# A memset of its own between one box gather and the next on GpSimd

## The chip, the cores and the metric

The kernel runs on one core of a Trainium2 chip. The metric is device time in microseconds (us) of one execution. The engines are named as the profile names them: PE is TensorE's matmuls and PEld its weight loads, DVE is VectorE, ACT is ScalarE, POOL is GpSimd, SP is SyncE, which only issues transfers.

## The reference

Four convolution layers run one after the other on an image batch x of shape (4, 48, 256, 256). Each layer gets the normalised output of the one before and adds its input again. Cut to what matters here:

```python
# layer 0: 1x1 conv, 3x3 depthwise conv, product of q and k in the 8x8 Fourier domain, norm, 1x1 conv
# layer 1: 1x1 conv, mask in the 8x8 Fourier domain, 3x3 depthwise conv, gelu gate, 1x1 conv
# layer 2 (boxes):
integ = jnp.cumsum(jnp.cumsum(x, axis=-1), axis=-2)          # integral image
off_w, off_h, scale = ...                                    # from two small conv branches
A  = _grid_sample_border_bilinear(integ, off_tl)             # four corners of a box per pixel,
Bt = _grid_sample_border_bilinear(integ, off_tr)             # each a blend of 4 neighbours
Ct = _grid_sample_border_bilinear(integ, off_bl)
D  = _grid_sample_border_bilinear(integ, off_br)
return (A + D - Bt - Ct) / area
# layer 3: 1x1 conv, 3x3 depthwise conv, gelu gate, 1x1 conv, mask in the 8x8 Fourier domain
```

The corners of layer 2's boxes depend on the data, so their values are fetched from a table in device memory by index.

## The kernel before, in words

The 4 images are handled one at a time and an image is cut into 32 strips of 8 rows. For each image the program runs layer 0, layer 1, the integral image (written to memory as a table) and the front of layer 2, which computes for every pixel the table indices, the 16 blend weights and the reciprocal of the area and spills them to memory. Tiles of these stages have names that begin with `a_`, `b_`, `i_` and `c_`. Layer 3, with names `d_`, runs for all 4 images at the end.

The rest of layer 2, the box part (names `e_`, class `Boxes`), has no stage of its own. It is woven into other stages: the boxes of image 0 into layers 0 and 1 of image 1, those of image 1 into image 2's, those of image 2 into image 3's, and those of image 3 into layer 3 of images 0 to 2. Layer 0 and layer 1 of image 0, and layer 3 of image 3, have no boxes in them.

The box part works in units of 512 pixels, 128 units for an image, 64 in each layer 0 or layer 1 and 128 in the three box-carrying images of layer 3. For one unit:

- GpSimd issues 16 indirect DMAs (`gather` at L1674, `gather_unit` at L1689), each with one index per partition, into one of `nb` buffers `got`. `nb` is 2 in layers 0 and 1 and 4 in layer 3. GpSimd may start a unit when VectorE has finished the unit `nb` before it (semaphore `used`).
- VectorE waits for the 16 gathers (semaphore `gathered`), multiplies by the weights (L1727, twice), adds halves (L1733 twice, L1739, L1741, the last frees the buffer) and multiplies by the reciprocal area (L1744). These instructions stand at fixed places in VectorE's program between those of the host layer.
- TensorE transposes the result (L1769), VectorE adds the residual and takes statistics (L1782, L1784), SyncE stores it.

Every engine runs its own program in order. The engines meet only at semaphores and at the barrier between blocks (one block for each layer of each image). GpSimd has little else to do: some clears at a block's start (L875, L878), loads for the integral image (L1211) and the spills (L1417 to L1424). SyncE issues all other transfers; all transfers of the core, GpSimd's too, use the same 16 DMA engines. `ALU` rows in the listings below are register arithmetic.

Of the kernel before, what the change touches and what calls it, by code (L numbers as in the profile page):

```python
# [29 lines left out]
WIDE = 66  # L30
NPROD = 94
CREDIT = 8


def stack_planes():
# [104 lines left out]
def allocators(nc, ctx, tag):  # L140

    def sb(name, shape, dt=F32):
        return ctx.enter_context(nc.sbuf_tensor(f"{tag}_{name}", shape, dt))

    def pb(name, shape=(128, 512)):
        return ctx.enter_context(nc.psum_tensor(f"{tag}_{name}", list(shape), F32))
    return sb, pb


def semaphores(env, tag, names):  # L150


    keys = [("all" if n == "turn" else tag, n) for n in names]
    for k in keys:
        if k not in env.sems:
            env.sems[k] = env.ctx.enter_context(env.nc.semaphore("_".join(k)))
    return [env.sems[k] for k in keys]


def planes(t, b, c0, cn, row, rows, col=0, cols=WP):  # L160

    return t[ds(b, 1), c0:c0 + cn, ds(row, rows), col:col + cols].rearrange("a c y x -> (a c) y x")
# [108 lines left out]
def credit(eng, *sems, n=1):  # L271

    for s in sems:
        eng.sem_inc(s, n * CREDIT)

# [34 lines left out]
def first_stats(env, src, stats):  # L310
# [3 lines left out]
    with ExitStack() as ctx:  # L314
# [4 lines left out]
        with nc.Block() as block:  # L319
            @block.sync  # L320
            def _(sp):
                with sp.Fori(0, S // 2) as u:
                    for k in range(2):

                        sp.wait_ge(used, u * 2 + k + CREDIT - 1)
                        sp.dma_start(x[k][:], planes(src, 0, 0, CP, (u * 2 + k) * SROWS + 1, SROWS)).then_inc(loaded[k], 16)
# [13 lines left out]
def layer0(env, src, dst, p, b, boxes=None, stats=None):  # L340
# [6 lines left out]
    with ExitStack() as ctx:  # L347
# [37 lines left out]
        if stats is not None:  # L385
# [5 lines left out]
            loads_before = [U, U] + [0] * (B - 3)  # L391
        n_first = b * (4 * S) + CREDIT

        def pipeline(eng, begin, step):

            n0 = b * (4 * S) + CREDIT
            begin(n0)
# [16 lines left out]
        with nc.Block() as block:  # L416
            @block.sync
            def _(sp):
# [16 lines left out]
                def strip(u, k, load, more):  # L435
                    s = u * 2 + k
                    if more and stats is not None:
                        for i, t in enumerate(others):
                            sp.wait_ge(others_used, CREDIT + S + s * (B - 1) + i + 1)
                            sp.sem_inc(turn, 1)  # L440
                            sp.dma_start(t[:], planes(src, i + 1, 0, CP, (s + 1) * SROWS + 1, SROWS)).then_inc(others_loaded[i], 16)
                    if load:

                        sp.wait_ge(qk_ready, 2 * ((b * S + s + 1) * NQ + CREDIT))
                        sp.sem_inc(turn, 1)
# [882 lines left out]
class Spill:  # L1328


    def __init__(self, env):
        self.idx = env.nc.dram_tensor("spill_idx", [env.B, env.S, 128, NT * 4], I32, kind="Internal").ap()
        self.wt = env.nc.dram_tensor("spill_wt", [env.B, env.S, 128, NT * 16], F32, kind="Internal").ap()
        self.rec = env.nc.dram_tensor("spill_rec", [env.B, env.S, 128, NT * C], F32, kind="Internal").ap()
# [249 lines left out]
class Boxes:  # L1584
# [8 lines left out]
    def __init__(self, env, ctx, src, dst, table, spill, b, nb, ni):  # L1593
        self.env, self.src, self.dst, self.spill, self.b, self.nb, self.ni = env, src, dst, spill, b, nb, ni
        self.flat = table.rearrange("x y c -> (x y c)").rearrange("(n o) -> n o", o=1)
        sb, _ = allocators(env.nc, ctx, f"e{b}")
        self.got = [sb(f"got{i}", [128, 4, 4 * REC]) for i in range(nb)]
        self.idx = [sb(f"idx{i}", [128, self.HT * 4], I32) for i in range(ni)]
        self.wt = [sb(f"wt{i}", [128, self.HT * 16]) for i in range(2)]
        self.rec = [sb(f"rec{i}", [128, self.HT, C]) for i in range(2)]  # L1600
        self.out = [sb(f"out{i}", [CP, self.HROWS, WP]) for i in range(2)]
        self.box = sb("box", [128, 4, C])
        self.val = [sb(f"val{i}", [128, 4, WIDE]) for i in range(2)]
        (self.halved, self.used, self.v_ready, self.y_ready, self.res_ready, self.stats_done, self.turn_sem, self.cleared,
         aux0, aux1, x0, x1, s0, s1) = semaphores(env, "e", [
             "halved", "used", "v_ready", "y_ready", "res_ready", "stats_done", "turn", "cleared",
             "aux_loaded0", "aux_loaded1", "x_loaded0", "x_loaded1", "stored0", "stored1"])
        self.aux_loaded, self.x_loaded, self.stored = [aux0, aux1], [x0, x1], [s0, s1]
        self.idx_loaded = semaphores(env, "e", [f"idx_loaded{i}" for i in range(ni)])
        sems = semaphores(env, "e", [f"gathered{i}" for i in range(2 * nb)])  # L1610
        self.gathered = [sems[2 * i:2 * i + 2] for i in range(nb)]
        self.n0 = b * (4 * env.S) + CREDIT

        self.filled = [b * (2 * env.S) if i < 2 else 0 for i in range(nb)]
        self.listed = [b * env.S if i < 2 else 0 for i in range(ni)]
# [40 lines left out]
    def stores_done(self, sp, e):  # L1656
        for i in range(2):
            sp.wait_ge(self.stored[i], (self.b * self.env.S + e + 1) * 16)

    def gather(self, pool, lo, hi):  # L1660

        per = self.ni // 2
        with pool.Fori(lo // per, hi // per) as v:
            for slot in range(self.ni):
                pool.wait_ge(self.idx_loaded[slot], (self.listed[slot] + v + 1) * 16)
                for j in range(2):
                    q = (2 * slot + j) % self.nb

                    pool.wait_ge(self.used, self.n0 + v * (2 * self.ni) + (2 * slot + j) - self.nb + 1)
                    pool.sem_inc(self.turn_sem, 1)  # L1670
                    for t in range(4):
                        for c in range(4):
                            at = (j * 4 + t) * 4 + c
                            pool.indirect_dma_start(out=self.got[q][:, t, c * REC:(c + 1) * REC], out_offset=None, in_=self.flat,  # L1674
                                                    in_offset=bass.IndirectOffsetOnAxis(ap=self.idx[slot][:, at:at + 1], axis=0)
                                                    ).then_inc(self.gathered[q][t // 2], 16)

    def gather_unit(self, pool, v, at):

        slot, j = divmod(at, 2)  # L1680
        q = at % self.nb
        pool.wait_ge(self.idx_loaded[slot], (self.listed[slot] + v + 1) * 16)
        pool.sem_inc(self.turn_sem, 1)
        pool.wait_ge(self.used, self.n0 + v * (2 * self.ni) + at - self.nb + 1)
        pool.sem_inc(self.turn_sem, 1)
        for t in range(4):
            for c in range(4):
                col = (j * 4 + t) * 4 + c
                pool.indirect_dma_start(out=self.got[q][:, t, c * REC:(c + 1) * REC], out_offset=None, in_=self.flat,  # L1689
                                        in_offset=bass.IndirectOffsetOnAxis(ap=self.idx[slot][:, col:col + 1], axis=0)  # L1690
                                        ).then_inc(self.gathered[q][t // 2], 16)

    def gather_units(self, pool, lo, hi):

        per = 2 * self.ni
        first, last = -(-lo // per), hi // per
        for n in range(lo, min(hi, first * per)):
            self.gather_unit(pool, n // per, n % per)
        if last > first:
            with pool.Fori(first, last) as v:  # L1700
                for at in range(per):
                    self.gather_unit(pool, v, at)
        for n in range(max(lo, first * per, last * per), hi):
            self.gather_unit(pool, n // per, n % per)
# [560 lines left out]
```

## Time and profile before

| what | value |
|---|---|
| time, median of 3 runs | 25,575.53 us (25,561.85 to 25,586.71) |
| span of the profiled execution | 30,534.6 us (no other time of this execution is given) |
| PE busy in it | 26,188.2 us, 86% |
| DVE busy | 15,839.1 us, 52% |
| ACT busy | 7,030.3 us, 23% |
| POOL busy | 9,431.4 us, 31% |
| indirect gathers | 8192, 6144 at L1674 and 2048 at L1689 |
| bytes moved by DMA | 2,256 MB, 74 GB/s over the span |

The profiled execution is 19% longer than the median of the runs. Times of single rows come from the profiled execution, and so a sum of stages in it is not the time of a run. The share of a busy engine is a mean over stages that differ: the stages with gathers and those without have to be read apart.

### The profile page before, as it was taken

What the parts mean: (1) busy time and instruction counts of PE and PEld (TensorE: products, weight loads), DVE (VectorE), ACT (ScalarE), POOL (GpSimd) and SP (SyncE); (2) the same over time, 40 slices, a digit from 0 to 9 for tenths busy, and PEclk for the clock granted to TensorE, in tenths of its full rate; (3) what the DMA queues carried; (4) which work ended last, traced back from release to release, by engine and by line L of the source; (5) the groups of instructions that cost most, each with busy time, mean ns of one, the idle gap of its engine ahead of it and who ended that gap; (6) DMA issues with size and microseconds to landing.
All of it is one profiled execution on the core that took longest, in us unless ns stands there. A gap on an engine that the chain in (4) does not pass through costs nothing. (4 is left out here: it accounts for less than half of the span.)

```text
span 30534.6 us, 424064 instructions
## 1 busy us (share of the span) xinstructions
PE 26188.2 (86%) x147480; PEld 17011.4 (56%) x147480; DVE 15839.1 (52%) x23975; ACT 7030.3 (23%) x13096; POOL 9431.4 (31%) x8564
## 2 busy tenths in 40 slices
PE   7999988777799988777799988777799988888889
PEld 5765564555544464555544464555444464666667
DVE  4445555444466655444466645444466655555553
ACT  2333321222222211222222211222222211211222
POOL 0000000333344311333344401333344403767740
PEclk9999989888888879888888879888888878989999
DMA  3220014333222224333222224333222234655543
GB/s 77 58 46 20 20 52 112 68 71 71 57 59 62 58 75 107 70 68 69 57 60 59 60 77 104 68 70 68 57 60 59 61 86 114 129 118 124 128 102 73
DMA packets 875573, 2256.01 MB, mean 74 GB/s; under 512 B 257480, under 2 KB 509132, under 8 KB 762800
## 3 DMA queue, kind: packets, MB, share of 16 engines
q1 hardware_dynamic: 454512, 1309.67, 18.7%
q0 software_dynamic: 419840, 928.94, 12.2%
q8 instruction: 902, 14.78, 0.2%
q14 instruction: 319, 2.61, 0.0%
HBM read 1860.59 MB, written 385.13 MB: 74 GB/s over the span
## 5 line engine op out<-in xcount | busy, mean ns | idle before, releaser
L1674 POOL DMA_INDIRECT e_got<-table,e_idx x6144 | 6363.5, 1036 | 10224.3 <-DVE e_box L1741 8206.1
L1689 POOL DMA_INDIRECT e_got<-table,e_idx x2048 | 2780.0, 1357 | 1031.7 <-issue 659.4
L1078 DVE TENSOR_TENSOR b_ym<-b_p_f,b_mask 128x304 f32<-128x304 f32 x2112 | 999.8, 473 | 3821.8 <-PE b_p_f L900 2295.2
L283 PE MATMUL d_p<-d_xs,d_ws 125*96 125x512 f32 x9216 | 2542.9, 419 | 230.6 <-issue 205.8
L1092 DVE SCALAR_TENSOR_TENSOR b_acc<-b_z,b_dwc,b_acc 112x1024 f32<-112x1024 f32 x2112 | 2620.0, 1277 | 4.2
L1021 ACT ACTIVATE b_ys<-b_p_in 128x304 f32<-128x304 f32 x2112 | 894.7, 424 | 7181.5 <-PE b_p_in L953 5191.7
L512 PE MATMUL a_p_qk<-a_wst,a_stack 125*128 125x192 f32 x12288 | 2459.7, 336 | 69.2 <-issue 45.8
L923 PE MATMUL b_p_conv<-b_z,b_diag_e 32*32 32x512 f32 x19008 | 2221.0, 689 | 182.7 <-issue 168.6
L923 PE MATMUL b_p_conv<-b_z,b_diag_a 64*64 64x512 f32 x19008 | 2341.1, 613 | 1.5 <-issue 0.8
L689 DVE RECIPROCAL a_rs<-a_sd 128x4 f32<-128x4 f32 x512 | 89.5, 175 | 4098.8 <-ACT a_sd L613 4059.4
L512 PEld LDWEIGHTS a_p_qk<-a_wst,a_stack 125*128 125x128 f32 x12288 | 2055.5, 194 | 155.6 <-issue 70.5
L907 PEld LDWEIGHTS b_p_z<-const,b_ym 128*66 128x66 f32 (+2 forms) x12672 | 1743.9, 179 | 640.0 <-issue 154.6
L907 PE MATMUL b_p_z<-const,b_ym 128*66 128x128 f32 (+2 forms) x12672 | 1890.8, 287 | 161.5 <-ACT b_z L1009 114.3
L283 PEld LDWEIGHTS d_p<-d_xs,d_ws 125*96 125x96 f32 x9216 | 1496.4, 168 | 858.5 <-issue 287.1
L953 PE MATMUL b_p_in<-b_w,b_xt 66*128 66x304 f32 x4224 | 1706.7, 487 | 250.7 <-issue 198.8
L1727 DVE TENSOR_TENSOR e_got<-e_got,e_wt 128x1536 f32<-128x1536 f32 x1024 | 1763.0, 1745 | 123.6 <-DMA e_got<-table,e_idx 109.8
L953 PEld LDWEIGHTS b_p_in<-b_w,b_xt 66*128 66x128 f32 x4224 | 706.2, 203 | 1655.4 <-issue 1574.9
L560 PE MATMUL a_p_c<-a_conv,const 96*96 96x512 f32 x1024 | 649.7, 721 | 1120.9 <-ACT a_conv L599 789.5
L283 PE MATMUL a_p_v<-a_xs,a_ws 125*96 125x512 f32 x4608 | 1598.2, 498 | 0.0
L900 PE MATMUL b_p_f<-b_ys,const 128*128 128x304 f32 x4224 | 1540.7, 446 | 33.6 <-issue 29.0
L306 PE MATMUL c_p_g<-c_stack,c_wst 125*96 125x512 f32 x3072 | 1431.4, 602 | 24.8 <-issue 24.8
L1733 DVE TENSOR_TENSOR e_got<-e_got 128x1536 f32<-128x1536 f32 (+1 forms) x1024 | 1386.7, 1354 | 24.2
(274 smaller groups left out, 40407.6 us busy)
## 6 DMA issues: line engine op xcount, KB each, us to landing
e_got<-table,e_idx POOLq DMA_INDIRECT x8192
a_stack<-in_xp SPq DMA_DIRECT2D x256, 387.0 KB
c_stack<-planes SPq DMA_DIRECT2D x256, 387.0 KB
d_stack<-planes SPq DMA_DIRECT2D x256, 387.0 KB
table<-i_acc SPq DMA_DIRECT2D x256, 384.0 KB, 2.3
b_x<-planes SPq DMA_DIRECT2D x132, 395.1 KB
b_xr<-planes SPq DMA_DIRECT2D x264, 197.5 KB
planes<-b_out SPq DMA_DIRECT2D x264, 197.5 KB
```

Source lines behind the costliest of these rows:

```text
L283: pe.matmul(out, ws[i][:, dx, lo:hi], xs[j][:, r0:r0 + QROWS, dx:dx + W], start=(dx == i == j == 0), stop=False)
L306: pe.matmul(out, wst[:, dx, lo:hi], stack[:, r0:r0 + QROWS, dx:dx + W], start=(dx == 0), stop=False)
L512: pe.matmul(dst_, st[:, row, dx + 128 * t:dx + 128 * t + 128], wst[:, dx, 0:2 * C2], start=(dx == 0), stop=False)
L900: pe.matmul(p_f[:, 0:NC], env.c("dft"), ys[k % 2][:], start=True, stop=True).then_inc(f_ready, 1)
L907: mm = pe.matmul(p_z[g][0:MZ[g], k % 4 * 128:k % 4 * 128 + 128], ym[k % 2][:, LO[g]:LO[g] + MZ[g]], env.c("idft"), start=True, stop=True)
L923: mm = pe.matmul(p_conv[r][size * c:size * (c + 1), :], diag[size * r:size * (r + 1), k, :], zs[g][size * r:size * (r + 1), QROWS * q + dy ...
L953: pe.matmul(p_in[:, 0:NC], xt[par][:, t, :], w[:], start=True, stop=True).then_inc(in_ready, 1)
L1092: dve.scalar_tensor_tensor(out=a, in0=rows, scalar=dwc[0:M[D], D, k:k + 1], in1=a, op0=ALU.mult, op1=ALU.add).then_inc(chain, 1)
L1674: pool.indirect_dma_start(out=self.got[q][:, t, c * REC:(c + 1) * REC], out_offset=None, in_=self.flat, in_offset=bass.IndirectOffsetOnAxi ...
L1689: pool.indirect_dma_start(out=self.got[q][:, t, c * REC:(c + 1) * REC], out_offset=None, in_=self.flat, in_offset=bass.IndirectOffsetOnAxi ...
L1727: dve.tensor_tensor(part, part, self.wt[i][:, at:at + 32].unsqueeze(2).broadcast_to([128, 32, C]), ALU.mult).then_inc(self.halved, 1)
L1733: dve.tensor_tensor(got[:, :, 0:half], got[:, :, 0:half], got[:, :, half:2 * half], ALU.add).then_inc(self.halved, 1)
```

## The change

GpSimd gets a tile `beat` of one partition with 600 float32 elements and a semaphore `rested`. After each indirect gather it waits until its clear after the gather before has completed and then clears `beat` again; the completion adds one to `rested`. The very first wait is met by an increment at the start. Nobody but GpSimd reads or waits for either. The 8192 gathers are followed by 8192 clears; everything on the other engines stays as it is.

```diff
+BEAT = 600
...
+        self.beat = sb("beat", [1, BEAT])
...
+    def rest(self, pool, unit, k):
+
+        pool.wait_ge(self.rested, (unit + (self.n0 - CREDIT)) * 16 + (k + 1))
+        pool.sem_inc(self.turn_sem, 1)
+        pool.memset(self.beat[:], 0.0).then_inc(self.rested, 1)
+
     def gather(self, pool, lo, hi):
 
+        if self.b == 0 and lo == 0:
+            pool.sem_inc(self.rested, 1)
...
                             pool.indirect_dma_start(out=self.got[q][:, t, c * REC:(c + 1) * REC], out_offset=None, in_=self.flat,
                                                     in_offset=bass.IndirectOffsetOnAxis(ap=self.idx[slot][:, at:at + 1], axis=0)
                                                     ).then_inc(self.gathered[q][t // 2], 16)
+                            self.rest(pool, v * (2 * self.ni) + (2 * slot + j), 4 * t + c)
...
+                self.rest(pool, v * (2 * self.ni) + at, 4 * t + c)
```

On GpSimd, in the loop of `gather` inside layer 0 of image 1, the program before has this at the first unit's gathers (`e_used` is the semaphore that frees a buffer, `e_idx_loaded0` that of the index list):

```order
L1663 ISA
L1669 ISA [waits e_idx_loaded0]
L1674 DMA e_got<-table,e_idx 128x192 [waits e_used]
L1674 DMA e_got<-table,e_idx 128x192 x15
L1669 REGISTER_ALU
```

and the changed one has this:

```order
L1679 ISA [waits e_idx_loaded0]
L1684 DMA e_got<-table,e_idx 128x192 [waits e_used]
L1664 ISA
L1666 MEMSET e_beat 1x600 [waits e_rested]
L1684 DMA e_got<-table,e_idx 128x192
L1664 REGISTER_ALU
L1666 MEMSET e_beat 1x600 [waits e_rested]
L1684 DMA e_got<-table,e_idx 128x192
```

The 16 gathers of a unit no longer follow one another; between two of them stand one register instruction (the value to wait for) and the clear with its wait.

On GpSimd in layer 3's loop of `gather_unit`, before:

```order
L1684 ISA
L1689 DMA e_got<-table,e_idx 128x192 x16
L1684 REGISTER_ALU
L1689 DMA e_got<-table,e_idx 128x192 x16
L1684 REGISTER_ALU
```

and after the change, at the end of one unit and the start of the next:

```order
L1700 DMA e_got<-table,e_idx 128x192
L1664 REGISTER_ALU
L1666 MEMSET e_beat 1x600 [waits e_rested]
L1695 REGISTER_ALU [waits e_idx_loaded1]
L1700 DMA e_got<-table,e_idx 128x192 [waits e_used]
L1664 ISA
L1666 MEMSET e_beat 1x600 [waits e_rested]
L1700 DMA e_got<-table,e_idx 128x192
```

Here too each gather is followed by a clear, the last one of a unit as well, so that it stands ahead of the next unit's first gather.

## Rows read from the trace of the kernel before

**Rows 1.** Page: busy us, share of the span, instructions; then tenths in 40 slices.

```profile
PE 26188.2 (86%) x147480; PEld 17011.4 (56%) x147480; DVE 15839.1 (52%) x23975; ACT 7030.3 (23%) x13096; POOL 9431.4 (31%) x8564
...
POOL 0000000333344311333344401333344403767740
PEclk9999989888888879888888879888888878989999
```

**Rows 2.** Stretches (start:end us, length, busy by engine, granted clock, DMA): one stage each.

```profile
186.00:2137.00 1951.00, 1913.45 (x11268) 1489.90 (x11268) 891.81 (x1543) 720.27 (x1408) 0.00 (x0) 1.00 0.26 58
2167.00:4247.00 2080.00, 2013.45 (x15316) 1067.36 (x15315) 1219.90 (x1652) 671.70 (x1219) 15.86 (x9) 0.97 0.07 20
...
5280.00:8145.00 2865.00, 2195.50 (x11780) 1668.99 (x11778) 1211.62 (x1735) 722.20 (x1409) 1003.48 (x1024) 0.85 0.31 68
8163.00:11000.00 2837.00, 2590.24 (x15828) 1255.42 (x15828) 1762.86 (x2229) 669.62 (x1219) 1136.04 (x1033) 0.85 0.21 58
...
25616.00:29410.00 3794.00, 3216.28 (x16335) 2384.72 (x16336) 2121.56 (x2851) 742.03 (x1315) 2775.69 (x2048) 0.90 0.58 124
29510.00:30530.00 1020.00, 1000.35 (x5254) 754.61 (x5254) 367.67 (x587) 256.71 (x449) 0.00 (x0) 0.98 0.34 75
```

**Rows 3.** Order of time, layer 1 of image 1: PE while gathers run.

```profile
8475.00 4.24 PE L923 MATMUL b_p_conv<-b_z,b_diag_e 32*32 32x512 f32 x42
...
8479.60 3.36 PE L923 MATMUL b_p_conv<-b_z,b_diag_e 32*32 32x512 f32 x6 [0.35 <-issue]
...
8480.07 0.95 POOL L1674 DMA_INDIRECT e_got<-table,e_idx  x1 [0.30 <-issue]
...
8481.33 0.96 POOL L1674 DMA_INDIRECT e_got<-table,e_idx  x1 [0.30 <-issue]
```

**Rows 4.** Groups by line (busy us, mean ns | idle before, releasers): gathers, transposes.

```profile
L1674 POOL DMA_INDIRECT e_got<-table,e_idx x6144 | 6363.5, 1036 | 10224.3 <-DVE e_box L1741 8206.1 <-issue 1918.5 <-DMA e_idx<-spill_idx 99.7
L1689 POOL DMA_INDIRECT e_got<-table,e_idx x2048 | 2780.0, 1357 | 1031.7 <-issue 659.4 <-DVE e_box L1741 372.3
...
L1769 PE MATMUL b_p_y<-const,e_val 128*66 128x128 f32 x1536 | 297.0, 344 | 38.4 <-issue 37.7
...
L1769 PE MATMUL a_p_c<-const,e_val 128*66 128x128 f32 x1536 | 201.0, 274 | 0.0
...
L1769 PE MATMUL d_p_c<-const,e_val 128*66 128x128 f32 x1024 | 130.4, 276 | 20.0 <-DVE d_out L2091 16.0 <-issue 3.6
```

**Rows 5.** Groups by line: GpSimd's clears.

```profile
L878 POOL MEMSET b_z<- 64x2580 f32 x8 | 17.9, 2243 | 0.0
...
L878 POOL MEMSET b_z<- 128x2580 f32 x8 | 17.9, 2243 | 0.0
...
L875 POOL MEMSET b_xr<- 128x1032 f32 x4 | 3.8, 955 | 0.0
L875 POOL MEMSET b_w<- 66x304 f32 x4 | 1.4, 350 | 0.0
```

**Rows 6.** Order of time, layer 3 of image 0: two long gathers, and DVE.

```profile
26220.24 5.74 POOL L1689 DMA_INDIRECT e_got<-table,e_idx  x1 [0.30 <-issue]
...
26221.74 3.41 DVE L1727 TENSOR_TENSOR e_got<-e_got,e_wt 128x1536 f32<-128x1536 f32 x2
...
26226.28 4.37 POOL L1689 DMA_INDIRECT e_got<-table,e_idx  x1 [0.30 <-issue]
```

**Rows 7.** Order of time, layer 0 of image 1: a unit blended, then the next gather.

```profile
6176.06 3.40 DVE L1727 TENSOR_TENSOR e_got<-e_got,e_wt 128x1536 f32<-128x1536 f32 x2
...
6182.88 0.36 DVE L1741 TENSOR_TENSOR e_box<-e_got 128x192 f32<-128x192 f32 x1
...
6184.05 0.94 POOL L1674 DMA_INDIRECT e_got<-table,e_idx  x1 [24.19 <-DVE e_box L1741]
```

**Rows 8.** Order of time, layer 1 of image 1: first and last step of a blend.

```profile
8932.74 1.75 DVE L1727 TENSOR_TENSOR e_got<-e_got,e_wt 128x1536 f32<-128x1536 f32 x1
...
8948.08 0.36 DVE L1741 TENSOR_TENSOR e_box<-e_got 128x192 f32<-128x192 f32 x1
```

More of the change, by code:

```diff
@@ L1602, in __init__ @@
         self.box = sb("box", [128, 4, C])
+        self.beat = sb("beat", [1, BEAT])
         self.val = [sb(f"val{i}", [128, 4, WIDE]) for i in range(2)]
-        (self.halved, self.used, self.v_ready, self.y_ready, self.res_ready, self.stats_done, self.turn_sem, self.cleared,
+        (self.rested, self.halved, self.used, self.v_ready, self.y_ready, self.res_ready, self.stats_done, self.turn_sem, self.cleared,
          aux0, aux1, x0, x1, s0, s1) = semaphores(env, "e", [
-             "halved", "used", "v_ready", "y_ready", "res_ready", "stats_done", "turn", "cleared",
+             "rested", "halved", "used", "v_ready", "y_ready", "res_ready", "stats_done", "turn", "cleared",
              "aux_loaded0", "aux_loaded1", "x_loaded0", "x_loaded1", "stored0", "stored1"])
```

## The prediction, made before the changed kernel ran

> **What bounds the kernel now.** I read the page first. PE is busy for 86% of the span, POOL for 31%, and POOL only from slice 8 on [rows 1]. A mean of 31% says nothing yet, since POOL's digit is 3 or 4 in the first layers and 7 in the last one. So next I cut the span into stages and compared each with its twin: the same stage with and without gathers [rows 2]. Layer 0 without boxes takes 1951 us and layer 1 2080 us, with PE busy for 98% and 97%. With boxes the same stages take 2865 and 2837 us, although PE has hardly more to do. In order of time one sees PE fall from 42 matmuls in 4.24 us to 6 in 3.36 us, at nobody's semaphore, while POOL issues a gather every 1.25 us [rows 3].
>
> Is that stall there in a run without the profiler? The median time says mostly not. The nine stretches with gathers exceed their twins by 914, 950 and 938 us (layer 0 of images 1 to 3; the row of image 1 stands for three), by 757, 758 and 748 us (layer 1) and by 834 us in layer 3 (25616 to 30530 is 4914 us against 4 x 1020 us): together 5899 us. The span without them is 30,535 - 5899 = 24,636 us. The boxes' transposes add 201 + 297 + 130 = 628 us of PE [rows 4], which makes 25,264 us. The median of the runs is 25,575 us, only 311 us more. So I take it that in a plain run PE sets the pace nearly everywhere, and that nearly all of the 4959 us between the span and the median are PE's stalls beside gathers under the profiler. The sum is therefore made against this rebuilt execution and the median, not by scaling the span.
>
> **How much time POOL has for a unit.** From the same rows, for a plain run: layer 0 with boxes 1951 + 67 (a third of 201) = 2018 us for 64 units, 31.5 us each. Layer 1 has 2080 + 99 = 2179 us, 34.0 us each. Layer 3 with boxes has 3 x 1020 + 130 = 3190 us for 128 units, 24.9 us each.
>
> **How much it needs.** A gather's own row is 0.980 us in layer 0 (1003.48 / 1024), 1.094 us in layer 1 (1136.04 less 15.9 of clears, by 1024) and 1.357 us in layer 3 [rows 2, 4]. Behind each stands 0.30 us in which it waits for nothing shown [rows 3, 7]. Sixteen of them: 20.5 us, 22.4 us and 26.6 us. In layers 0 and 1 a third of the time is left. In layer 3 POOL needs 26.6 us where PE would give 24.9, so there POOL may already be the bound: 128 x 1.7 = 215 us, which is most of the 311 us that were left over. The trace speaks for this too: L1689's idle time is 659 us of issue and only 372 us of waiting for a free buffer, against 8206 us of such waiting at L1674 [rows 4].
>
> **What the change adds.** The clear of 1 x 600: a clear of 304 elements takes 350 ns and one of 1032 takes 955 ns, 0.831 ns an element; the number of partitions does not count, since 64 and 128 partitions both take 2243 ns [rows 5]. So 350 + 296 x 0.831 = 596 ns. The wait on `rested` is for the clear before, which ended before the gather in between began; I cost it and the register instruction at nothing, since both can be done while the gather runs; were they not, their price would be part of the gap below. Whether the clear brings an issue gap of its own no row shows: between clears the idle time is 0.0, between gathers 0.30 us. The bounds are 0 and 0.30 us; I take 0, the nearer row being the clears' [rows 5]. Behind the waiting clear are queued all later gathers, and for those VectorE waits at L1727, with its whole layer and then PE behind it.
>
> Layer 3: 16 x 0.596 = 9.5 us a unit on an engine that is the bound or within 10% of it. From 26.6 to 36.1 us, on 128 units: +1221 us. All of it is on the path: four buffers delay the trouble by four units, no more.
>
> Layers 0 and 1: 20.5 + 9.5 = 30.1 us against 31.5, and 22.4 + 9.5 = 32.0 us against 34.0. POOL just fits. Two buffers are enough for it: a buffer's cycle is two units, 63 us, of which its own gathers take 30 and the blend 7 (6176 to 6183) in layer 0, and 32 and 16 of 68 us in layer 1, so the gathers can run end to end [rows 7, 8]. I cost these stages at nothing; what hides the clears is POOL's wait for the freed buffer, 24.19 us in the row [rows 7]. If 0.1 us more per gather came on top, this cover would be gone in layer 0.
>
> Part of the clear may be absorbed. Some gathers last 4 to 6 us, and they lie beside VectorE's additions and products with both inputs in SBUF: 5.74 us beside a pair of L1727 [rows 6]. When such a hold begins during a clear, the clear runs on and the gather loses less.
>
> The Trainium skill ("SBUF — State Buffer", Who interferes with whom) says that a VectorE instruction with two SBUF inputs contends with a GpSimd instruction that reads SBUF, not with one that only writes it, and that tensor_tensor was not seen to stall descriptor generation. The long rows speak against the second half; no run here shows the first half for a clear. By it the excess of a gather in layer 3, (1.357 - 0.95) x 16 = 6.5 us a unit, would shrink by about a tenth, and the sum would be near 1130 us instead of 1221.
>
> I leave this out of the sum, since a PE that waits also spends time at the lower of its two levels (1.2 instead of 2.4 GHz): the granted clock is 0.85 in the stretches with stalls, against 0.97 to 1.00 without [rows 2], which costs something on the other side. The forecast is 25,576 + 1221 = 26,797, said as 26,800 us. Its own range: if the unprofiled gather in layer 3 has no holds, POOL needs 20.0 us before and 29.6 after, 4.7 over 24.9, +602 us: 26,180. At the other end a third of the larger gap in all stages: 27,400.
>
> **Rivals.**
> Gap: each clear costs 0.90 us, because the 0.30 us come after it as well. Layer 3 then gets +1221 + 16 x 0.30 x 128 = +1840 us. Layer 0 needs 35.0 us against 31.5, layer 1 36.8 against 34.0: 64 x 3 x (3.5 + 2.8) = +1210 us. Together 28,630 us. For it: every gather has that gap, whatever stands around it. Against: clears have none.
>
> Relief (faster): the stall of rows 3 exists in plain runs too and is caused by gathers that follow one another without a break. A break of 0.6 us lets the others through. At most the 311 us over the rebuilt sum can be won, and only if POOL keeps up in layer 3, that is if a gather with its clear takes under 24.9 / 16 = 1.56 us in a plain run; from there on it loses again. With two thirds won: 25,370 us. For it: the stall stands beside gathers alone, and stages without them have none. Against: the median leaves little room for it.
>
> The Trainium skill ("DMA: Bandwidth & Descriptors", Issuing engines are not separate DMA queues) says that transfers of all issuing engines interleave on the same 16 DMA engines, which would be a way for gathers to hold up others. Rows 2 show these engines at 0.21 to 0.58 busy in such stretches.
>
> Hidden (no change): in a plain run a gather takes so much less than 1.25 us that the clear fits in everywhere. The profiler may lengthen POOL's rows as it does PE's issue. Then 25,580 us. The condition is the same 1.56 us, with nothing to win.
>
> **How the numbers follow.** POOL becomes the bound in layer 3, as forecast: 0.68. Gap, in whole or in part: 0.15. Relief: 0.08. Hidden: 0.09. The range is to hold 8 in 10. Down it reaches from 26,180 into the ground between Hidden and the forecast, to 25,950; up it takes in about half of Gap, to 28,000. Left out are Relief, most of Hidden and the full Gap. A difference under 0.2% (51 us) can't be told from no change; by the cases the time is slower by more with 0.84, within it with 0.08, faster with 0.08.
>
> **What would show it.** Right: in layer 3 with boxes the time from one gather to the next is 1.85 us or more, POOL waits for L1741 hardly at all, VectorE's L1727 waits for gathers by hundreds of us, and the stretch grows from 3794 us towards 128 x 36 = 4600 us. A clear's row is near 596 ns, with 0.0 before it. In layers 0 and 1 POOL's wait for L1741 shrinks by about 9.5 us a unit and VectorE does not wait. Gap shows in the idle time before the clear and the gather after it. Relief shows if layers 0 and 1 with boxes get shorter and PE's slow stretches go. Wrong at the root would be that L1727 does not wait in layer 3, or that its stretch stays as long as it was.

## The result, and the profile after

| | before | changed |
|---|---|---|
| time, median | 25,568.69 us (4 runs, 25,546.63 to 25,586.71) | 26,636.92 us (4 runs, 26,622.66 to 26,652.27) |
| ratio | | 1.0425, 95% interval 1.0413 to 1.0437 |

The change costs 1068 us; 1221 were forecast (26,800 us, range 25,950 to 28,000). Busy shares and slices of the changed kernel's page, which answer to [rows 1]:

```profile
PE 24037.8 (90%) x147480; PEld 16338.0 (61%) x147480; DVE 15838.4 (59%) x23975; ACT 7045.7 (26%) x13096; POOL 15392.2 (58%) x16756
...
POOL 0000000099889920998899209988992199888930
PEclk9999997999999979999999799999997988888899
```

POOL's digits are now 8 and 9 in the stages with gathers, where they were 3 and 4, and 7 in the last layer [rows 1].

One thing has to be said first. The span of this profile is 26,621.1 us, the same as its time. The first profile of the kernel before, on which the prediction stands, was of an execution 5 ms longer than every other one of that kernel. Profiled a second time that kernel has a span of 25,539.8 us, and PE's slow stretches of [rows 3] are gone. They were that one execution's own; no later profile showed them again, and their cause stays open. From here on "before" is this second profile. Its stretches (columns as in [rows 2]): layer 0 and layer 1 of image 1, layer 3 with boxes, layer 3 of image 3:

```profile
5269.00:7284.00 2015.00, 1964.62 (x11778) 1543.00 (x11778) 1210.40 (x1740) 721.05 (x1408) 1031.70 (x1024) 0.99 0.45 98
7302.00:9450.00 2148.00, 2069.00 (x15820) 1120.96 (x15820) 1759.73 (x2223) 671.91 (x1219) 1284.25 (x1036) 0.97 0.29 77
20930.00:24490.00 3560.00, 3172.14 (x16763) 2403.22 (x16764) 2164.95 (x2923) 765.67 (x1344) 2793.72 (x2048) 0.94 0.64 134
24490.00:25525.00 1035.00, 995.90 (x5244) 751.23 (x5242) 375.37 (x598) 257.75 (x450) 0.00 (x0) 0.97 0.34 75
```

and the same four in the changed kernel:

```profile
5277.00:7329.00 2052.00, 1971.50 (x11780) 1549.89 (x11780) 1209.74 (x1736) 722.26 (x1409) 1828.22 (x2048) 0.99 0.44 96
7347.00:9556.00 2209.00, 2087.45 (x15828) 1125.72 (x15828) 1767.79 (x2228) 672.35 (x1219) 1949.48 (x2057) 0.97 0.27 75
...
21221.00:25590.00 4369.00, 3326.93 (x16790) 2497.89 (x16790) 2167.84 (x2934) 767.86 (x1346) 3839.07 (x4096) 0.87 0.51 109
25590.00:26616.00 1026.00, 1000.74 (x5254) 755.73 (x5254) 370.12 (x589) 256.84 (x449) 0.00 (x0) 0.98 0.34 75
```

The prediction had rebuilt 2018 and 2179 us for layers 0 and 1; they are 2015 and 2148. The loss has two parts. Layer 3 goes from 4599 us to 5394 us, +795. The three layers 0 together give +113 us and the three layers 1 +148 us, where nothing was forecast. The groups that answer to [rows 4] in the changed kernel, with all clears of the program, the gathers of layer 3 (L1700) and VectorE's first step of a blend in all stages:

```profile
L1666 POOL MEMSET e_beat<- 1x600 f32 x8192 | 4822.4, 589 | 0.3
L1700 POOL DMA_INDIRECT e_got<-table,e_idx x2048 | 2642.5, 1290 | 498.1 <-POOL e_beat L1666 344.4
L1739 DVE TENSOR_TENSOR e_got<-e_got,e_wt 128x1536 f32<-128x1536 f32 x1024 | 1779.8, 1749 | 1712.6 <-DMA e_got<-table,e_idx 1710.3
```

and before:

```profile
L1689 POOL DMA_INDIRECT e_got<-table,e_idx x2048 | 2793.7, 1364 | 742.4 <-issue 663.0 <-DVE e_box L1741 79.4
...
L1727 DVE TENSOR_TENSOR e_got<-e_got,e_wt 128x1536 f32<-128x1536 f32 x1024 | 1770.4, 1746 | 624.0 <-DMA e_got<-table,e_idx 620.9 <-issue 0.3
```

Over the whole program VectorE's wait for gathers grows from 621 to 1710 us, about as much as the time. In layer 3 alone, before and then changed (total, times, longest):

```profile
DVE e_got L1727 <- DMA e_got<-table,e_idx: 560.0, 95, 19.8
```

```profile
DVE e_got L1739 <- DMA e_got<-table,e_idx: 1354.7, 185, 22.9
```

This wait grows by 795 us, as much as the stage. It was 560 us before the change already: GpSimd was late then too. In order of time, layer 3 of the changed kernel:

```profile
23025.83 0.59 POOL L1666 MEMSET e_beat<- 1x600 f32 x1
23027.16 0.95 POOL L1700 DMA_INDIRECT e_got<-table,e_idx  x1 [0.75 <-POOL e_beat L1666]
23028.12 0.59 POOL L1666 MEMSET e_beat<- 1x600 f32 x1
23028.87 0.95 POOL L1700 DMA_INDIRECT e_got<-table,e_idx  x1 [0.16 <-POOL e_beat L1666]
23029.82 0.59 POOL L1666 MEMSET e_beat<- 1x600 f32 x1
23030.01 1.76 DVE L1739 TENSOR_TENSOR e_got<-e_got,e_wt 128x1536 f32<-128x1536 f32 x1 [16.89 <-DMA e_got<-table,e_idx]
...
23032.99 1.64 PE L1977 MATMUL d_p_b<-d_ys,const 128*128 128x392 f32 x2 [10.79 <-DVE d_ym L2094]
```

The clear starts when the gather ends, and the next gather 0.16 us after the clear (0.75 us in one of these rows; 0.163 us is the median of the 2048). VectorE has waited 16.89 us for the unit's data, and PE 10.79 us for VectorE.

### The profile page after: what moved, and what is told of

Read it like the earlier page. It is cut to its first block and busy times, and to the rows that moved or that the text cites. A ratio compares the mean times of both kernels' runs of the same rounds, so it can differ in the third digit from the quotient of the medians.

```text
span 26621.1 us, 448385 instructions
## 1 busy us (share of the span) xinstructions
PE 24037.8 (90%) x147480; PEld 16338.0 (61%) x147480; DVE 15838.4 (59%) x23975; ACT 7045.7 (26%) x13096; POOL 15392.2 (58%) x16756
## 5 line engine op out<-in xcount | busy, mean ns | idle before, releaser
L1684 POOL DMA_INDIRECT e_got<-table,e_idx x6144 | 7672.7, 1249 | 1211.8 <-POOL e_beat L1666 1004.2
L1666 POOL MEMSET e_beat<- 1x600 f32 x8192 | 4822.4, 589 | 0.3
L1700 POOL DMA_INDIRECT e_got<-table,e_idx x2048 | 2642.5, 1290 | 498.1 <-POOL e_beat L1666 344.4
L1212 POOL DMA_DIRECT2D i_x<-planes x128 | 66.3, 518 | 3776.6 <-issue 2412.4
L908 PEld LDWEIGHTS b_p_z<-const,b_ym 128*66 128x66 f32 (+2 forms) x12672 | 1658.9, 172 | 431.2 <-issue 36.5
L908 PE MATMUL b_p_z<-const,b_ym 128*66 128x128 f32 (+2 forms) x12672 | 1783.7, 277 | 13.0 <-ACT b_z L1010 12.9
L954 PE MATMUL b_p_in<-b_w,b_xt 66*128 66x304 f32 x4224 | 1623.9, 467 | 152.0 <-issue 147.7
L901 PE MATMUL b_p_f<-b_ys,const 128*128 128x304 f32 x4224 | 1474.1, 430 | 121.1 <-DVE b_ym L1079 121.1
L284 PE MATMUL a_p_v<-a_xs,a_ws 125*96 125x512 f32 x4608 | 1369.0, 441 | 0.0
```

The source lines that it names most:

```text
L284: pe.matmul(out, ws[i][:, dx, lo:hi], xs[j][:, r0:r0 + QROWS, dx:dx + W], start=(dx == i == j == 0), stop=False)
L901: pe.matmul(p_f[:, 0:NC], env.c("dft"), ys[k % 2][:], start=True, stop=True).then_inc(f_ready, 1)
L908: mm = pe.matmul(p_z[g][0:MZ[g], k % 4 * 128:k % 4 * 128 + 128], ym[k % 2][:, LO[g]:LO[g] + MZ[g]], env.c("idft"), start=True, stop=True)
L954: pe.matmul(p_in[:, 0:NC], xt[par][:, t, :], w[:], start=True, stop=True).then_inc(in_ready, 1)
L1666: pool.memset(self.beat[:], 0.0).then_inc(self.rested, 1)
```

## The experiments

Nine kernels ran beside the changed one, the kernel before among them. Each ratio is to runs of the kernel before on the same chip, whose medians lie between 25,541 and 25,569 us. The time with clears of 1200 is from two runs, the others from four or more. Stage lengths are from a stage's first to its last matmul, in us; for layers 0 and 1 the mean of images 1 to 3.

| kernel | time | ratio, 95% interval | layer 0 | layer 1 | layer 3 |
|---|---|---|---|---|---|
| before (stages: second profile) | 25,553 | | 2015 | 2152 | 4599 |
| changed | 26,637 | 1.0425, 1.0413 to 1.0437 | 2053 | 2201 | 5394 |
| clears in layers 0, 1 only | 25,859 | 1.0117, 1.0101 to 1.0132 | 2050 | 2215 | 4585 |
| clears in layer 3 only | 26,351 | 1.0313, 1.0297 to 1.0329 | 2017 | 2149 | 5389 |
| clears of 1 element | 25,663 | 1.0044, 1.0030 to 1.0057 | 2018 | 2151 | 4683 |
| half the gathers in layer 3, no clears | 25,196 | 0.9859, 0.9843 to 0.9876 | 2018 | 2151 | 4240 |
| clears of 300 | 26,018 | 1.0184, 1.0167 to 1.0201 | 2020 | 2151 | 5050 |
| 16 clears behind the unit | 27,847 | 1.0897, 1.0879 to 1.0915 | 2194 | 2394 | 5614 |
| 4 clears of 2400 behind the unit | 26,379 | 1.0325, 1.0308 to 1.0342 | 2016 | 2179 | 5340 |
| clears of 1200 | 29,935 | 1.1720, 1.1696 to 1.1743 | 2455 | 2650 | 6181 |

**The kernel before once more.** No edit but a comment.

```diff
-REC = 4 * C
+REC = 4 * C  # as before
```

> The kernel before once more, for a second profile. Theory (the 30,535 us of its first profiled execution were that execution's own; layers 0 and 1 with boxes take 2017 and 2145 us in a plain run, as in the two experiments that leave their gathers unbroken there or nearly so): the time is 25,550 us and the span the same, with layer 0 at 2017, layer 1 at 2145 and the whole of layer 3 at 4585 us. Rival (gathers without a break in all stages slow PE down wherever a profile is taken): a span of 30,500 us again.

Measured: 25,553 us, ratio 1.0000 (0.9990 to 1.0009), span 25,539.8 us. The rival is out: in this profile gathers without a break do not slow PE down.

**Clears in layers 0 and 1 only.**

```diff
 def gather_unit(...)
-                self.rest(pool, v * (2 * self.ni) + at, 4 * t + c)
```

> Clears only behind the 6144 gathers of layers 0 and 1; layer 3 as before. Theory (all of the +1068 us arises in layer 3, where GpSimd is the bound): 25,570 us, within 60 us of the kernel before, and layers 0 and 1 with boxes at 2050 and 2200 us in the profile as in the changed kernel. Rival (the clears cost time everywhere, in proportion to their number): three quarters of 1068 us, 26,370 us.

Measured: 25,859 us. My theory that all of the loss is in layer 3 falls, and so does the rival: 0.3 of it is in layers 0 and 1. In layer 0 of image 1 the gathers' group before the change, and gathers and clears in the changed kernel:

```profile
L1674 POOL DMA_INDIRECT e_got<-table,e_idx x1024 | 1031.7, 1008 | 944.2 <-DVE e_box L1741 592.7 <-issue 351.5
```

```profile
L1684 POOL DMA_INDIRECT e_got<-table,e_idx x1024 | 1230.6, 1202 | 217.6 <-POOL e_beat L1666 169.6 <-issue 48.0
L1666 POOL MEMSET e_beat<- 1x600 f32 x1024 | 601.9, 588 | 0.0
```

GpSimd no longer waits for a buffer (592.7 us before, none now), and the mean gather has grown from 1.008 to 1.202 us. A unit takes 16 x (1.202 + 0.588) + 217.6 / 64 = 32.0 us, against the 2015 / 64 = 31.5 us that PE leaves. So GpSimd is full here as well. In layer 1 of image 1 it waited 451.6 us for a buffer before and does not wait for one in the changed kernel; the mean gather goes from 1.235 to 1.302 us.

**Clears in layer 3 only.** The other call is removed, and the wait counts from image 3's units.

```diff
 def gather(...)
-                            self.rest(pool, v * (2 * self.ni) + (2 * slot + j), 4 * t + c)
...
 def rest(...)
-        pool.wait_ge(self.rested, (unit + (self.n0 - CREDIT)) * 16 + (k + 1))
+        pool.wait_ge(self.rested, unit * 16 + (k + 1))
```

> Clears only behind the 2048 gathers of layer 3. Theory: the whole loss, 26,600 to 26,640 us, with the stretch of layer 3 with boxes at 4370 us. Rival (in proportion): 25,840 us. Second question: if the stalls of PE in layers 0 and 1 belong to the profiler and to gathers without a break, the span of the profile is longer than the time again, by about 4000 us.

Measured: 26,351 us, between the theory and the rival. Layer 3 is as expected: 5389 us in all, 5 less than in the changed kernel. The two halves, +310 and +802 us over the before of the same chip, add up to the loss of the whole within 44 us. The span was 26,339.6 us: the second question is answered with no.

**Clears of 1 element.**

```diff
-BEAT = 600
+BEAT = 1
```

> All 8192 clears, of 1 element instead of 600. Theory (only the time on GpSimd counts): a clear of about 0.10 us plus 0.16 us before the next gather takes the place of the 0.30 us idle before each gather, so a gather recurs every 1.21 us instead of 1.25 us, and the time is that of before or up to 80 us less: 25,490 to 25,570 us. Rival (the wait on a semaphore and the extra instruction have a fixed price of 0.1 us or more each time): 25,569 + 2048 x 0.1 = 25,770 us or more.

Measured: 25,663 us, +114 us, between what the two expected. Layer 3 is 84 us longer, layers 0 and 1 are as before. In order of time, layer 3:

```profile
22001.36 0.95 POOL L1700 DMA_INDIRECT e_got<-table,e_idx  x1 [0.22 <-POOL e_beat L1666]
22002.31 0.09 POOL L1666 MEMSET e_beat<- 1x1 f32 x1
22002.61 0.95 POOL L1700 DMA_INDIRECT e_got<-table,e_idx  x1 [0.22 <-POOL e_beat L1666]
```

The clear takes 0.09 us and the next gather starts 0.22 us later, so gathers recur every 1.25 us exactly as without clears (0.95 + 0.30). A clear this short is free, it stands in a pause that is there anyway; the gain I had expected does not exist. The +114 us are elsewhere. GpSimd's idle stretches over 2 us in layer 3 add up to 175 us against 79 us before, and besides the two at block starts (34 and 44 us) there are eleven of 6 to 14 us, each ahead of a unit whose number is a multiple of 8, where a pass of the loop begins. The instruction queue q14 fetched 411 packets instead of 319. Two other kernels bear out that this is GpSimd's longer program: with clears in layers 0 and 1 only (328 packets) the eleven are not there, nor with the 4 clears a unit tried below (325 packets). No run changed the program's length alone.

**Half the gathers in layer 3, without clears.** The buffers are cleared once before the first gather of layer 3, and the output of image 3's boxes is computed with two of four corners missing. A first version, without that clearing, gave no time; 25,350 to 25,440 us had been expected of it, from the 130 to 215 us that GpSimd was then thought to cost.

```diff
 def gather_unit(...)
-            for c in range(4):
+            for c in range(2):
...
 def weigh(...)
-        dve.wait_ge(self.gathered[q][h], (self.filled[q] + fills + 1) * 128)
+        dve.wait_ge(self.gathered[q][h], self.filled[q] * 128 + (fills + 1) * (64 if self.nb == 4 else 128))
...
+                    if b == 0:
+                        for g_ in boxes.got:
+                            pool.memset(g_[:], 0.0).then_inc(boxes.fresh, 1)
+                        pool.wait_ge(boxes.fresh, 4)
```

> The kernel before with 8 of the 16 gathers of every unit of layer 3 left out and the buffers cleared once ahead of it, so that image 3's boxes are computed from partly missing corners. Theory (GpSimd already was the bound of layer 3 before the change): the boxes' stretch falls from about 3560 to about 3230 us, the time to 25,220 us. Rival (PE set layer 3's pace and GpSimd just kept up): no change, 25,550 us.

Measured: 25,196 us, 353 us less than before and as the theory said; layer 3 is 359 us shorter. The gathers of layer 3 now wait for buffers:

```profile
L1690 POOL DMA_INDIRECT e_got<-table,e_idx x1024 | 1549.8, 1514 | 1553.1 <-DVE e_box L1742 1242.0 <-issue 311.1
```

1242 us against 79 before. So GpSimd was the bound of layer 3 before the change; this is shown, and 353 us is what halving its gathers gives back. A unit of layer 3 now takes (4240 - 1035) / 128 = 25.0 us (1035 us is the last image, without boxes), the pace that the prediction had rebuilt for PE (24.9).

**Clears of 300 elements.**

```diff
-BEAT = 600
+BEAT = 300
```

> All 8192 clears, of 300 elements. Theory (a gather recurs after max(0.305, clear + 0.157) us of pause; only a stage where GpSimd is full pays): a clear of 0.34 us, so 0.50 us of pause instead of 0.305 us, +0.19 x 2048 = +400 us in layer 3 and nothing in layers 0 and 1, where GpSimd is full only from a pause of about 0.7 us on: 25,950 us. Rival (each clear costs its own length wherever it stands): half of 1068 us in all stages, 26,080 us, with layers 0 and 1 at 2035 and 2175 us.

Measured: 26,018 us, about as far from the theory's time as from the rival's, so the stages decide. Layers 0 and 1 are as before (2020 and 2151 us); the rival, which wants them at 2035 and 2175, is out. Layer 3 is +451 us where 400 were expected, and 52 us of that are again long idle stretches (131 us against 79). GpSimd still waits for buffers in layer 0 of image 1, so it is not full there:

```profile
L1684 POOL DMA_INDIRECT e_got<-table,e_idx x1024 | 1079.6, 1054 | 561.2 <-DVE e_box L1753 346.9 <-POOL e_beat L1666 154.4 <-issue 59.9
```

**16 clears behind the unit instead of one behind each gather.**

```diff
-                self.rest(pool, v * (2 * self.ni) + at, 4 * t + c)
+        for k in range(16):
+            self.rest(pool, v * (2 * self.ni) + at, k)
...
```

`gather` is changed in the same way.

> The same 8192 clears of 600 elements, but the 16 of a unit all behind its 16th gather. Theory (GpSimd's sum counts, and a clear between two gathers hides 0.15 us of the pause that gathers have among themselves): 16 x 0.15 = 2.4 us more a unit than in the changed kernel, +300 us in layer 3 and up to +150 us in each layer 1: 26,900 to 27,200 us. Rival (what costs is that the gathers are stretched out and meet more of VectorE's holds): 26,640 us or less, nearer to 26,300 us if the holds fall back to those of before in layers 0 and 1.

Measured: 27,847 us, far over both. In order of time:

```profile
23305.31 0.59 POOL L1666 MEMSET e_beat<- 1x600 f32 x1 [0.15 <-POOL e_beat L1666]
23306.05 0.59 POOL L1666 MEMSET e_beat<- 1x600 f32 x1 [0.15 <-POOL e_beat L1666]
23306.79 0.59 POOL L1666 MEMSET e_beat<- 1x600 f32 x1 [0.15 <-POOL e_beat L1666]
23307.74 2.90 POOL L1701 DMA_INDIRECT e_got<-table,e_idx  x1 [0.36 <-issue]
23310.94 0.95 POOL L1701 DMA_INDIRECT e_got<-table,e_idx  x1 [0.30 <-issue]
```

A clear that waits for the clear right before it starts 0.15 us after that one's end. Between gathers this wait costs nothing, since a gather lies between; in a row it is 2.3 us a unit (15 times 0.154), which the theory had not counted, and the gathers have their 0.30 us back, which it had. Layer 3:

```profile
L1701 POOL DMA_INDIRECT e_got<-table,e_idx x2048 | 2260.2, 1104 | 804.9 <-issue 725.8 <-DVE e_box L1755 79.1
L1666 POOL MEMSET e_beat<- 1x600 f32 x2048 | 1203.9, 588 | 302.1 <-POOL e_beat L1666 302.0
```

Against the changed kernel GpSimd idles 307 us more before gathers and 302 us more before clears, and the gathers take 382 us less, since their mean fell to 1.104 us: +227 us, where the stage shows +220. So the rival's point, fewer holds, is there too, but smaller than the pauses.

**4 clears of 2400 elements behind the unit.**

```diff
-BEAT = 600
+BEAT = 2400
...
-        for k in range(16):
+        for k in range(4):
...
```

The lines are against the kernel with 16 clears behind the unit; the values waited for count by 4 instead of 16.

> Behind a unit's 16 gathers 4 clears of 2400 elements (a clear of 2.09 us) instead of 16 of 600: the same number of elements a unit, 12 semaphore waits fewer. Theory (the lump of 16 was slow because each clear waits 0.15 us for the one before it; without that, clears outside the gathers cost GpSimd less than between them, since its gathers meet fewer of VectorE's holds): 8.4 + 3 x 0.15 = 8.8 us of clears instead of 11.8 us, 32.4 us a unit in layer 3, layers 0 and 1 near 2030 and 2170 us: 26,300 us. Rival (clears behind the unit are slow because the next unit's gathers start later than they could): 27,500 us or more, as with 16 clears.

Measured: 26,379 us, 1468 us less than with 16 clears in a row, and layer 0 is back at 2016 us. The theory's 26,300 us was within 0.3%, and the rival is out. The clears of a unit take 8.4 us with 3 waits where they took 9.4 us with 15: 2.9 us less, of which the waits are 1.8. Fewer clears and fewer waits were not tried apart. By stages the theory was less exact: 32.4 us a unit and the last image make 5180 us for layer 3, and it took 5340. A gather takes 1.078 us in layer 0 of image 1 and 1.192 us in layer 3.

**Clears of 1200 elements.**

```diff
-BEAT = 600
+BEAT = 1200
```

> All 8192 clears, of 1200 elements (1.09 us). Theory (GpSimd is the bound of every stage with gathers, at 16 x (0.95 + 1.09 + 0.157) us and 3.5 to 5.5 us of holds a unit): 39 us a unit in layer 0, 40 us in layer 1, 41 to 42 us in layer 3; stages of 2540, 2670 and 6400 us: 30,400 us. Rival (the waits of the changed kernel in layers 0 and 1 are irregular and do not mean that GpSimd is full): layers 0 and 1 grow by clearly less than 500 us each, the time stays under 29,500 us.

Measured: 29,935 us. The two stretches of image 1 (columns as in [rows 2]):

```profile
5270.00:7730.00 2460.00, 2104.51 (x11722) 1707.51 (x11722) 1210.29 (x1733) 719.36 (x1404) 2237.42 (x2048) 0.90 0.36 81
7745.00:10400.00 2655.00, 2256.24 (x15810) 1196.16 (x15810) 1765.37 (x2225) 670.32 (x1218) 2401.91 (x2060) 0.88 0.23 62
```

0.5 us more for each of 1024 gathers is 512 us; layer 0 grew by 402 us over the changed kernel and layer 1 by 449, the rest going to gathers that were shorter (1.10 us in layer 0 where they were 1.20). Once GpSimd is full, a stage pays 79 to 88% of what is added. The rival's time, under 29,500 us, is out, though its other condition, growth of clearly less than 500 us in each of layers 0 and 1, is not ruled out by 402 us. The theory's 30,400 us was 465 us too long: it took 3.5 us of holds a unit or more, and layer 0 shows (1.10 - 0.95) x 16 = 2.4; layer 3 was 219 us shorter than it said.

## Why the prediction was right, and where not

*GpSimd is the bound of layer 3, and may have been before.* Right, and shown from both sides: with half the gathers 353 us less, with clears there alone +802 us. The forecast of 215 us for what GpSimd cost before was too small: a unit took (4599 - 1035) / 128 = 27.8 us and not 26.6. Sixteen gathers with their pauses are 26.7 us. Most of the rest is idle time at the starts of the three blocks (27, 33 and 45 us), which the sum left out: 0.8 us a unit.

*The clear takes 596 ns.* 589 ns.

*It brings no gap of its own, and the gathers keep their 0.30 us.* The mis-sized step. The pause between two gathers was 0.305 us and is 0.588 + 0.157 = 0.745 us (gathers recur every 1.698 us, and one takes 0.952): +0.44 us, not +0.596. The clear starts without a gap and hides half of the pause that the gathers had among themselves. The rival named Gap had the 0.30 us come once more; the 0.16 us behind the clear stand in their place. For layer 3: 0.44 x 2048 = +901 us. The gathers' mean fell from 1.364 to 1.290 us, -152 us, and the long idle stretches grew by 35 us: +784 us, where the stage shows +795 and the forecast said +1221.

*Part of the clear is absorbed by VectorE's holds.* It was named and left out of the sum; it is worth the 152 us, 12% of the forecast. The excess over 0.95 us fell from 6.6 to 5.4 us a unit, by nearly a fifth where a tenth had been estimated. Clears run on beside VectorE's work, as assumed. Clears and gathers of layer 3, min/median/max in ns:

```profile
L1700 POOL DMA_INDIRECT e_got<-table,e_idx x2048: 951/952/5807, 21248.6 to 25544.3; - x187
```

```profile
L1666 POOL MEMSET e_beat<- x2048: 587/588/594, 21249.6 to 25545.2; 1x600 f32 x187
```

Gathers are held for up to 4.9 us, clears of this layer never for more than 7 ns. The Trainium skill ("SBUF — State Buffer", Who interferes with whom) says that a VectorE instruction with two SBUF inputs does not contend with a GpSimd instruction that only writes SBUF. The trace agrees: 668 of the 2048 clears lie beside such an instruction, and the longest of them takes 594 ns. Where the page says that tensor_tensor was not seen to stall a DMA, the long gathers of [rows 6] differ, and the measurement decides.

The trace says more on the cause than those two rows. Before the change 858 of layer 3's 2048 gathers lie beside a VectorE instruction with both inputs in SBUF; they take 1.94 us in the mean and hold all of the excess. The other 1190 take 0.947 us, none more than 1.022, and 489 of them lie beside other work of VectorE. In layers 0 and 1 too over 99% of the excess lies beside such instructions. That is the trace's evidence; no run took these instructions away.

*Layers 0 and 1 cost nothing, GpSimd just fits.* Wrong: +261 us. The sum took the gather at the 0.980 us (layer 1: 1.094 us) of a GpSimd that was idle half the time, in an execution with stretched stages. The second profile shows 1.008 and 1.235 us; with 1.235 us the prediction's own sum makes 16 x (1.235 + 0.30 + 0.596) = 34.1 us for layer 1, and nothing is left of its 34.0. The step that failed is this: the length of a gather is not a constant of the instruction. With GpSimd idle between units most gathers ran outside VectorE's holds, and GpSimd waited instead for the buffer that VectorE's blend was about to free. Stretched over the whole period they meet more of them: in layer 0 of image 1, 371 of 1024 gathers lie beside an instruction with both inputs in SBUF, where 172 did. Over the 0.95 us of an undisturbed gather the excess rose from about 1 to 4 us a unit in layer 0. Put behind the unit, the same 9600 elements leave it at 2 us, and layer 0 loses nothing. With 300 elements there is still room, and nothing is lost either.

*The total.* The errors are of opposite sign: layer 3 cost 426 us less than forecast, layers 0 and 1 cost 261 us that were not. That the total came within 163 us is luck to that extent; each part is further off than the whole.

*PE's clock.* The term was left out of the sum. In layer 3 with boxes the granted clock falls from 0.94 to 0.87 and PE is busy for 155 us more with the same work. GpSimd's own sum accounts for the stage to 11 us, so no share of the loss is shown to be the clock's.

*Rebuilding a plain run from stages without gathers.* It gave the right pace (2018 and 2179 us against 2015 and 2148 measured). Its reading, that PE stalls beside gathers whenever it is profiled, was wrong: of ten profiles taken after it none shows it. Had the stall been scaled into the sum, layers 0 and 1 would have seemed to have 45 us a unit to spare for the clears.

*Relief and Hidden.* Relief needed PE's slow stretches in a plain run, and no profile whose span equals its time shows them. Both needed a plain gather far under 1.25 us, pause included; it takes 1.25 us in the second profile too.

## What to carry to other kernels

Compare what a queue needs for a unit of work with what its stage leaves, stage by stage; an engine that is busy for 31% of the span can be the bound of one stage and within a few per cent of it in others. When it fills up, take its instructions at the length they have on a full engine, since those that used to run in quiet stretches can now meet the others' holds. And a small instruction put into a pause costs what it lengthens the pause by, not its own length. When the profiled execution is far longer than the runs, rebuild the plain run from stages that are clean, or profile again, before anything is scaled.

## What was not expected of the hardware

Between two indirect gathers GpSimd pauses for 0.30 us; a clear between them starts at once and leaves 0.16 us behind it (0.22 us behind one of 1 element), so a clear of up to about 0.15 us (an estimate, 0.305 - 0.157) would be free; 0.09 us was. A clear that waits on the semaphore of the one right before it starts 0.15 us late, and not at all late with a gather between. A clear of one partition follows 0.087 + 0.000836 us an element from 1 to 2400 elements (0.09, 0.34, 0.589, 1.09, 2.09 us). In layer 1 some clears are held after all: with clears of 1 element 51 of 8192 last about 0.55 us instead of 0.09, and these are the 51 that begin while VectorE runs its multiply by a scalar into `b_acc` (one SBUF input). Longer code on GpSimd showed as idle stretches of 2 to 14 us where a pass of layer 3's loop begins.
